# Attention's end and routing in a fused attention and expert kernel: routing split 6 and 2, last softmax ahead of the choices, a second buffer for the last values

## The chip, the cores and the metric

The kernel runs on one core of one Trainium2 chip. The core has five engines that run side by side and wait for each other by semaphores: TensorE (PE, matrix products), VectorE (DVE), ScalarE (ACT), GpSimd (POOL) and SyncE (SP, which issues transfers). The metric is device microseconds of one execution; 2% is about what its measurement tells from no change. Three runs of the kernel before gave 464.08, 466.33 and 470.67 us, a median of 466.33.

## The reference, cut to what matters

One layer over 16 sequences of 64 tokens, 256 wide (1,024 tokens). First a gated attention with a self part and a cross part, whose concatenated values are rounded to an 8-bit grid and projected. Then a mixture of 16 experts, two per token, beside one shared expert:

```python
cat = jnp.concatenate([core, xout], axis=-1)
catq = _div_clamp_fp8(cat, proj_smooth)
...
logits = flat @ router_w.T
scores = jax.nn.softmax(logits, axis=-1)
_, topk_idx = jax.lax.top_k(logits + router_bias, TOPK)
...
out = out + combine[:, e:e + 1] * (h @ Wd[e])
...
x = x + jnp.tanh(g_xattn[0]) * _L0_xattn_ref(_layernorm(x, axis=-1), ctx_2048, ...)
x = x + jnp.tanh(g_ffn[0]) * _L0_ffn_ref(_layernorm(x, axis=-1), ...)
```

The change computes the same function in another order.

## The kernel before, in words

Tokens lie in 8 tiles of 128 rows (`NT`). Attention is 32 steps (`n = 4 t + c`): four for each tile, two of self and two of cross attention, each with four heads of keys and eight of queries. A step is a software pipeline over five engines: step n's projections and statistics, the heads of step n-1, the scores and softmax of step n-2, the values, smoothing and rounding ("quantisation") of step n-3, and the output product of step n-4 are in flight together. Steps of the tiles in the middle are one loop. The last tile's steps are written out (`run_steps`), and behind them each engine's program is a list by hand: the text of the program is the order in its queue. Nothing reorders it.

The names that matter, in the order of the data. `rows_out` (L787, ScalarE) writes a tile's normalised rows, the input of the experts; `late_rows` (L1453, VectorE) does it for tile 7. `z_transposes` (L1010, TensorE) and `z_out` (L772, ScalarE) turn them into columns. `router` (L1022) makes 16 logits per token. `route_top` (L1464 to L1476, VectorE) copies the logits, adds the bias, takes the maxima and their indices, and marks the chosen experts. `ranks` (L1031, L1035, L1040, TensorE) counts how many tokens before each one chose its expert, and `route_pos` (L1504 to L1509, VectorE) turns this into the slots of the token's two rows. `twin_rows` (L581, GpSimd) makes each row's second copy. `scatter` (L591, GpSimd) sends each tile's two copies to those slots of `zbuf` in HBM, one indirect transfer per copy. All this is done in two groups, tiles 0 to 6 and tile 7 (`GROUPS`); row statistics go by three (`ROWG`).

Attention's own end stands between them: `softmax_in` (L1344, L1347), `expo` (L724), `softmax_sum` (L1353, L1356), `normalise` (L554, GpSimd), `prob_transposes` (L968), `prob_copy` (L729), `values` (L982), `over_smooth` (L1363), `quantise` (L1295 to L1306), `output` (L992). `over_smooth` writes into one buffer, `yv`, that `quantise` clips in place, so the smoothing of one step waits behind the rounding of the step before. `root` in ScalarE's steps is `roots` (L696, L698), the inverse deviation of the heads' norm, for which GpSimd's coefficients wait. The last tile's rows need its `residual` (L1377), which needs the last `output`.

When tile 7's positions are known, `block_table` (L1515 to L1526) lists 32 blocks of 128 slots. SyncE waits for all 16 scatters and loads the blocks from `zbuf` in pairs (L458). A unit is one pair: `block_transposes` (L1138), `block_rows` (L804), `unit_up` (L1098), `unit_silu` (L797), `unit_hidden` (L1534), `unit_down` (L1110, L1113), `unit_out` (L1541, L1547), and two indirect transfers to `ybuf` on GpSimd (L614). Eight shared units, one for each tile, need no table; six of them stand ahead of the blocks. At the end the two expert rows per token are loaded back, weighted and added.

## Time and profile before

| What | Value |
|---|---|
| Median of 3 runs | 466.33 us (464.08 to 470.67) |
| The profiled execution | 469.92 us, span 468.1 us |
| Busy: TensorE / VectorE / ScalarE / GpSimd | 412.9 / 370.3 / 295.6 / 285.8 us |
| Mean granted TensorE clock | 0.968 of full |
| Attention's last written-out steps and end | about 322 to 373 us |
| Expert blocks | about 397 to 450 us |

The profile is of one execution. Busy time is the time of instructions, and idle time ahead of an instruction is printed with what released it. Times in the rows are us from the span's start.
### The profile page before, as it was taken

Reading aid. Unit: us, or ns where it says so; the run is one execution under the profiler, and the core shown is the slowest. Engines: PE = TensorE matmul, PEld = TensorE weight load, DVE = VectorE, ACT = ScalarE, POOL = GpSimd, SP = SyncE. Lnnn points to the kernel's source line nnn. Section 1 sums busy time; section 2 is a strip of 40 time slices with the busy share of each in tenths; the row PEclk is TensorE's granted clock in tenths of the full one; section 3 lists DMA queues with packets and bytes.
Section 4 is the critical chain, followed back from the end, with each engine's and each line's share of the span. In section 5 each row is a group of like instructions: output and inputs, shape, how many; then the busy total and the mean of one; then the engine's idle time right before and its main releaser. Section 6 shows DMA issues by size and latency. Waiting matters only on the chain.

```text
span 468.1 us, 10277 instructions
## 1 busy us (share of the span) xinstructions
PE 412.9 (88%) x3127; PEld 314.6 (67%) x3127; DVE 370.3 (79%) x824; ACT 295.6 (63%) x622; POOL 285.8 (61%) x409
## 2 busy tenths in 40 slices
PE   0677899999999999999999999999989587999970
PEld 0444567767776776776777677677779376999960
DVE  5878889999998999999989899999985844323347
ACT  4587967777766766767776677676882122666520
POOL 2079496586867759658686775964550662367750
PEclk9999999999999999999999999999997698999995
DMA  8940909999930000000000000000094122444317
GB/s 209 269 174 3 177 13 304 248 287 267 257 83 0 0 0 0 0 0 0 0 0 0 0 0 0 0 1 1 4 404 202 63 96 81 121 129 137 104 27 242
DMA packets 34812, 45.68 MB, mean 98 GB/s; under 512 B 3034, under 2 KB 32223, under 8 KB 33888
## 3 DMA queue, kind: packets, MB, share of 16 engines
q1 hardware_dynamic: 26656, 35.61, 26.1%
q0 software_dynamic: 6992, 9.46, 9.2%
q10 hardware_dynamic: 1136, 0.27, 0.3%
q8 instruction: 14, 0.23, 0.2%
q14 instruction: 14, 0.11, 0.1%
HBM read 28.34 MB, written 24.32 MB: 113 GB/s over the span
## 4 chain that ended last, share of the span: by engine, by line
PE 34%; DVE 19%; POOL 19%; issue 15%; ACT 8%; DMA 2%; ACTq 1%; POOLq 1%; another core or an unknown queue 1%; SPq 0%; DVEq 0%
PE proj_ps L933 9%; PE score_ps L960 7%; POOL ybuf L614 4%; PE out_ps L992 4%; PE pv_ps L982 4%; POOL rot L548 3%; POOL xin L520 3%; DVE st L1336 3%; DVE yv L1363 2%; ACT rot L684 2%; PE probT_ps L968 2%; POOL reg L554 2%; PE headT_ps L951 2%; ACT qT L719 2%; PE headT_ps L1098 1%
## 5 line engine op out<-in xcount | busy, mean ns | idle before, releaser
L933 PE MATMUL proj_ps<-arena 128*128 128x512 f16 x384 | 99.4, 382 | 6.7 <-POOL arena L522 3.9
L1336 DVE BATCH_NORM_STATS2 st<-rot 128x6 f32<-128x256 f32 x192 | 72.7, 420 | 14.5 <-ACT rot L684 13.3
L684 ACT ACTIVATE rot<-proj_ps 128x512 f32<-128x512 f32 x96 | 56.4, 587 | 22.2 <-PE proj_ps L933 20.6
L548 POOL TENSOR_TENSOR rot<-rot,cw 128x512 f32<-128x512 f32 x64 | 67.3, 1072 | 2.5
L554 POOL TENSOR_TENSOR reg<-reg,rinv 128x512 f32<-128x512 f32 x32 | 34.6, 1083 | 55.5 <-DVE rinv L1356 55.5
L960 PE MATMUL score_ps<-kT,qT 128*128 128x64 f32 x512 | 62.5, 276 | 0.6 <-ACT qT L719 0.5
L960 PEld LDWEIGHTS score_ps<-kT,qT 128*128 128x128 f32 x512 | 60.6, 194 | 2.4 <-ACT qT L719 2.2
L705 ACT ACTIVATE rot<-rot,cw 128x128 f32<-128x128 f32 x128 | 40.9, 390 | 30.3 <-POOL cw L542 30.3
L933 PEld LDWEIGHTS proj_ps<-arena 128*128 (+1 forms) x384 | 37.1, 102 | 32.5 <-issue 9.0
L925 PE MATMUL proj_ps<-arena 128*128 128x512 f16 x192 | 46.7, 379 | 0.6 <-POOL arena L507 0.6
L614 POOL DMA_INDIRECT ybuf<-arena,bslot x32 | 31.4, 983 | 18.5 <-issue 13.4
L982 PEld LDWEIGHTS pv_ps<-reg,vv 64*128 64x128 f32 x512 | 32.2, 193 | 14.5 <-issue 14.0
L1363 DVE TENSOR_TENSOR yv<-pv_ps,smi 128x512 bf16<-128x512 f32 x64 | 40.7, 678 | 0.0
L982 PE MATMUL pv_ps<-reg,vv 64*128 64x128 f32 x512 | 38.5, 291 | 1.9 <-DVE yv L1363 1.9
L951 PE MATMUL headT_ps<-idf,rot 128*128 128x128 f32 x256 | 38.5, 273 | 1.2 <-ACT kT L719 1.2
L992 PE MATMUL out_ps<-wp_sb,reg 128*128 128x256 bf16 x256 | 36.0, 287 | 3.7 <-DVE reg L1306 3.7
L724 ACT ACTIVATE reg<-reg 128x512 f32<-128x512 f32 x32 | 20.1, 628 | 24.4 <-DVE reg L1347 24.4
L951 PEld LDWEIGHTS headT_ps<-idf,rot 128*128 128x128 f32 x256 | 30.3, 140 | 7.4 <-issue 1.8
L536 POOL TENSOR_TENSOR nw<-vw,r 128x12 f32<-128x12 f32 x32 | 10.3, 321 | 37.3 <-ACT r L698 37.3
L992 PEld LDWEIGHTS out_ps<-wp_sb,reg 128*128 128x128 bf16 x256 | 23.5, 102 | 11.3 <-DVE reg L1306 4.5
L925 PEld LDWEIGHTS proj_ps<-arena 128*128 (+1 forms) x192 | 18.7, 98 | 16.2 <-issue 0.8
L719 ACT ACTIVATE qT<-headT_ps,colv 128x512 f32<-128x512 f32 x32 | 24.9, 779 | 0.1
(219 smaller groups left out, 874.2 us busy)
## 6 DMA issues: line engine op xcount, KB each, us to landing
zbuf<-fill SPq DMA_DIRECT2D x1, 16576.5 KB, 66.3
arena<-in_wffn SPq DMA_DIRECT2D x4, 1536.0 KB, 13.7
arena<-zbuf SPq DMA_DIRECT2D x32, 128.5 KB
wkv_stage<-in_wkvN SPq DMA_DIRECT2D x1, 2048.0 KB, 15.3
wp_sb<-in_wpT POOLq DMA_DIRECT2D x1, 2048.0 KB, 15.8
wp_sb<-ybuf SPq DMA_DIRECT2D x8, 256.0 KB, 5.4
xs<-in_x SPq DMA_DIRECT2D x2, 512.0 KB, 5.2
vv<-in_wqN POOLq DMA_DIRECT2D x1, 1024.0 KB, 12.6
```

Of the source, the lines that this page charges most:

```text
L548: gp.tensor_tensor(r, r, cw[:, 4 * i:4 * i + 4].unsqueeze(2).to_broadcast([P, 4, D]), ALU.mult)\
L554: gp.tensor_tensor(probn[s].rearrange("p (g t) -> p g t", t=S), prob[s].rearrange("p (g t) -> p g t", t=S), rinv[:, s, :].unsqueeze(2).to_ ...
L614: gp.indirect_dma_start(ybuf, bass.IndirectOffsetOnAxis(bslot[:, 2 * s + b:2 * s + b + 1], 0), yb[s % 3][:, b, :], None, bounds_check=TOPK ...
L684: act.activation(raw[c % 2][i], proj_ps[i % 2][:, :], ACT.Copy).then_inc(proj_evac, 1)
L925: mm = pe.matmul(ps, lhs, w[:, ch, o:o + 512], start=(k == 0), stop=(k == 5))
L933: mm = pe.matmul(ps, lhs, w[kind][:, ch, 512 * b:512 * b + 512], start=(k == 0), stop=(k == 3))
L951: mm = pe.transpose(dst, raw[c % 2][i][:, h * D:(h + 1) * D], idf[:, :])
L960: mm = pe.matmul(score_ps[:, (2 * g + b) * S:(2 * g + b + 1) * S], qT[:, s, 2 * g + b, :], kT[:, s, g, b * S:(b + 1) * S], start=True, sto ...
L982: mm = pe.matmul(pv_ps[b][:, g * P:(g + 1) * P], vv[rows, u, g * D:(g + 1) * D], pT[rows, g * P:(g + 1) * P], start=True, stop=True)
L992: mm = pe.matmul(out_ps[:, 0:H], catq[u % 2][:, h * P:(h + 1) * P], wp[:, 8 * u + h, :], start=(u == 0 and h == 0), stop=(u == NU - 1 and ...
L1336: ins = ve.bn_stats(st[:, 4 * i + h:4 * i + h + 2, :].rearrange("p h s -> p (h s)"), raw[c % 2][i][:, h * D:(h + 2) * D].rearrange("p (h d ...
L1363: ins = ve.tensor_tensor(y3[:, :, b * S:(b + 1) * S], pv_ps[b][:, :].rearrange("p (h t) -> p h t", t=S), smi[:, 8 * u:8 * u + 8].unsqueeze ...
```

## The change

Five things move, all at attention's end. The routing of tiles is split otherwise: the positions and scatters go by tiles 0 to 5 and 6 to 7 (`POSG`), the maxima and choices by 0 to 5, 6 and 7 (`TOPG`); tile 7's logits lie in another bank. `route_top` becomes `route_best` (copy, bias, maxima) and `route_choice` (indices, marks), with the last softmax's sum between them. The last step's smoothed values go into `xin`, an input buffer that is free by then. In ScalarE's last step the row outputs 3 to 5 move ahead of evacuations and the root ahead of two head evacuations. The queues of all engines behind the last step are reordered to fit. The weights of the two choices are computed once for all tiles, at the end.

```diff
@@ constants
-GROUPS = [(0, 7), (7, 8)]
+TOPG = [(0, 6), (6, 7), (7, 8)]
+POSG = [(0, 6), (6, 8)]
+HOME = 7
...
+        def logits_of(t0, t1):
+            return route_ps[:, t0:t1, :] if t1 < NT else out_ps[:, H:H + NE].unsqueeze(1)
@@ GpSimd
-            def twin_rows(g):
-
-                gp.wait_ge(rows_done, GROUPS[g][1])
-                gp.tensor_copy(zrow[g][:, :, 1, 0:H], zrow[g][:, :, 0, 0:H]).then_inc(twin_done, 1)
+            def twin_rows(t0, t1):
+
+                gp.wait_ge(rows_done, t1)
+                gp.tensor_copy(zrow[0][:, t0:t1, 1, 0:H], zrow[0][:, t0:t1, 0, 0:H]).then_inc(twin_done, 1)
...
-                gp.wait_ge(twin_done, g + 1)
+                gp.wait_ge(twin_done, 2 + g)
                 gp.wait_ge(pos_done, g + 1)
-                for t in range(*GROUPS[g]):
+                for t in range(*POSG[g]):
...
             run_steps(gp, step)
+            twin_rows(0, 6)
             normalise(last - 2, 0)
-            twin_rows(0)
+            twin_rows(6, 7)
             normalise(last - 1, 1)
@@ ScalarE, step(t, c)
+                final = isinstance(n, int) and n == NU * NT - 1
                 if attend:
                     expo(n - 2, c % 2)
+                if final:
+                    rows_out(3)
+                    rows_out(4)
                 if proj:
                     evacuate(n, c, 2)
...
                 if heads:
                     heads_out(n - 1, before, 0)
+                if final:
+                    rows_out(5)
                 if proj:
                     values_out(t, c)
...
+                if final:
+                    roots(n)
                 if heads:
                     heads_out(n - 1, before, 1)
                 if heads:
                     heads_out(n - 1, before, 2)
-                if proj:
+                if proj and not final:
                     roots(n)
@@ ScalarE, behind the steps
-            for t in range(3, 6):
-                rows_out(t)
             z_out(0)
+            z_out(1)
             prob_copy(last - 3, 1)
             norm_bank0(last - 1, 3)
-            z_out(1)
+            z_out(2)
             row_root(1)
+            heads_out(last - 1, 3, 0)
             expo(last - 2, 0)
+            heads_out(last - 1, 3, 1)
+            heads_out(last - 1, 3, 2)
             rows_out(6)
-            z_out(2)
-            for i in range(3):
-                heads_out(last - 1, 3, i)
             z_out(3)
             prob_copy(last - 2, 0)
             expo(last - 1, 1)
             act.preload_act_table_set("silu_and_others")
             unit_silu(0)
+            prob_copy(last - 1, 1)
             unit_silu(1)
-            prob_copy(last - 1, 1)
@@ TensorE, behind the steps
             scores(last - 2, 0)
+            z_transposes(2)
             values(last - 3, 1)
-            z_transposes(2)
             head_transposes(last - 1, 3, 0)
+            head_transposes(last - 1, 3, 1)
+            router(0, 4)
+            head_transposes(last - 1, 3, 2)
+            router(4, 6)
+            scores(last - 1, 1)
+            z_transposes(3)
+            prob_transposes(last - 2, 0)
             output(last - 4, 0, NT - 1)
-            head_transposes(last - 1, 3, 1)
-            head_transposes(last - 1, 3, 2)
-            z_transposes(3)
-            router(0, 6)
-            prob_transposes(last - 2, 0)
-            scores(last - 1, 1)
-            router(6, 7)
             values(last - 2, 2)
             output(last - 3, 1, NT - 1)
             shared_up(0)
-            shared_up(1)
-            ranks(0)
             prob_transposes(last - 1, 1)
             values(last - 1, 3)
+            ranks(0)
+            shared_up(1)
+            router(6, 7)
             output(last - 2, 2, NT - 1)
@@ VectorE
-            def over_smooth(w, u):
+            def over_smooth(w, u, y=yv):
...
-            def quantise(w, u):
+            def quantise(w, u, y=yv):
...
             softmax_in(last - 2, 0)
+            over_smooth(last - 3, 1)
             rows_scale(1)
             softmax_sum(last - 2, 0)
-            over_smooth(last - 3, 1)
             quantise(last - 3, 1)
             softmax_in(last - 1, 1)
-            route_top(0)
+            route_best(0)
             softmax_sum(last - 1, 1)
+            over_smooth(last - 2, 2)
+            route_choice(0)
+            ve.wait_ge(xgrid_done, NT)
+            over_smooth(last - 1, 3, xin)
             route_pos(0)
-            over_smooth(last - 2, 2)
             quantise(last - 2, 2)
-            over_smooth(last - 1, 3)
-            quantise(last - 1, 3)
+            quantise(last - 1, 3, xin)
...
             index_words(1)
+            route_best(1)
+            route_choice(1)
+            route_best(2)
+            route_choice(2)
             unit_out(0)
             unit_hidden(2)
-            route_top(1)
+            route_pos(1)
             unit_out(1)
-            route_pos(1)
             block_table()
```

TensorE's queue from the last head transposes on (`score_ps` as a target of L951 and L960 is heads and scores, `proj_ps` of L1022 the logits, `pv_ps` the values; the changed kernel's line numbers are 10 higher). Before:

```order
L951 MATMUL score_ps<-idf,rot 128x2x64 x4
L951 MATMUL headT_ps<-idf,rot 128x2x64 x4
L1010 MATMUL proj_ps<-idf,wkv_stage 128x128 x2
L1022 MATMUL proj_ps<-rws,xT 128x16 x12
L968 MATMUL probT_ps<-idf,reg 128x128 x4
L960 MATMUL score_ps<-kT,qT 128x64 x8
L1022 MATMUL proj_ps<-rws,xT 128x16 x2
L982 MATMUL pv_ps<-reg,vv 128x128 x8
L992 MATMUL out_ps<-wp_sb,reg 128x256 x8
L1098 MATMUL proj_ps<-xT,arena 128x128 x8
L1098 MATMUL headT_ps<-xT,arena 128x128 x8
```

Now:

```order
L961 MATMUL score_ps<-idf,rot 128x2x64 x4
L1032 MATMUL proj_ps<-rws,xT 128x16 x8
L961 MATMUL headT_ps<-idf,rot 128x2x64 x4
L1032 MATMUL proj_ps<-rws,xT 128x16 x4
L970 MATMUL score_ps<-kT,qT 128x64 x8
L1020 MATMUL proj_ps<-idf,wkv_stage 128x128 x2
L978 MATMUL probT_ps<-idf,reg 128x128 x4
L1002 MATMUL out_ps<-wp_sb,reg 128x256 x8
L992 MATMUL pv_ps<-reg,vv 128x128 x8
L1002 MATMUL out_ps<-wp_sb,reg 128x256 x8
L1108 MATMUL proj_ps<-xT,arena 128x128 x8
L978 MATMUL probT_ps<-idf,reg 128x128 x4
```

The last scores (L960, now L970) stand ahead of tile 6's transposes, of the other step's probabilities and of tile 6's logits; one shared unit of two stands ahead of the last transposed probabilities.

VectorE's queue from the last softmax's input on (`mx` and `sm` are its maximum and sum, `m`, `i` and `chosen` the routing's maxima, indices and marks). Before:

```order
L1344 TENSOR_REDUCE mx<-score_ps 128x8
L1347 TENSOR_TENSOR reg<-score_ps,mx 128x512
L1464 COPY arena<-proj_ps 128x112
L1465 TENSOR_TENSOR arena<-arena,rowv 128x112
L1468 MAX m<-arena 128x8 x7
L1471 MAX_INDEX i<-m,arena 128x8 x7
L1473 CAST i8f<-i 128x56
L1474 TENSOR_TENSOR arena<-rowv,i8f 128x224
L1476 TENSOR_TENSOR chosen<-arena 128x112
L1353 TENSOR_REDUCE sm<-reg 128x8
L1356 RECIPROCAL rinv<-sm 128x8
L1504 TENSOR_TENSOR arena<-arena,proj_ps 128x224
```

Now:

```order
L1355 TENSOR_REDUCE mx<-score_ps 128x8
L1358 TENSOR_TENSOR reg<-score_ps,mx 128x512
L1472 COPY arena<-proj_ps 128x96
L1473 TENSOR_TENSOR arena<-arena,rowv 128x96
L1476 MAX m<-arena 128x8 x6
L1364 TENSOR_REDUCE sm<-reg 128x8
L1367 RECIPROCAL rinv<-sm 128x8
L1374 TENSOR_TENSOR yv<-pv_ps,smi 128x8x64 x2
L1484 MAX_INDEX i<-m,arena 128x8 x6
L1486 CAST i8f<-i 128x48
L1487 TENSOR_TENSOR arena<-rowv,i8f 128x192
L1489 TENSOR_TENSOR chosen<-arena 128x96
L1374 TENSOR_TENSOR xin<-pv_ps,smi 128x8x64 x2
```

The sum and its reciprocal stand between the routing's maxima and its indices, for six tiles in place of seven, and both last smoothings (L1374) are ahead of the positions.

GpSimd's queue from the normalisation ahead of the twin copy on; a row outputs' second copy is `wkv_stage<-wkv_stage`, a scatter is a DMA to `zbuf`. Before:

```order
L554 TENSOR_TENSOR reg<-reg,rinv 128x512
L581 COPY wkv_stage<-wkv_stage 128x7x256
L554 TENSOR_TENSOR reg<-reg,rinv 128x512
L591 DMA zbuf<-wkv_stage,pos 16512x257 x14
L591 DMA zbuf<-arena,pos 16512x257 x2
```

Now:

```order
L585 COPY wkv_stage<-wkv_stage 128x6x256
L558 TENSOR_TENSOR reg<-reg,rinv 128x512
L585 COPY wkv_stage<-wkv_stage 128x256
L558 TENSOR_TENSOR reg<-reg,rinv 128x512
L595 DMA zbuf<-wkv_stage,pos 16512x257 x14
L595 DMA zbuf<-arena,pos 16512x257 x2
```

The copy of six tiles stands ahead of the normalisation, that of the seventh behind it. Of the 14 scatters from `wkv_stage`, 12 now belong to the first group and two, tile 6's, wait with tile 7's for the second positions.

## Rows read from the trace of the kernel before

**Rows 1.** Chain of waits, 399 to 468 us: start us, us, what.

```profile
404.12 0.42 POOL ybuf L614
...
449.39 0.98 POOL ybuf L614
```

**Rows 2.** TensorE in order of time: start, busy us, line, tiles, [idle, releaser].

```profile
348.91 2.75 PE L1022 MATMUL proj_ps<-rws,xT 128*128 128x16 f32 x24
...
351.98 2.90 PE L960 MATMUL score_ps<-kT,qT 128*128 128x64 f32 x16
...
361.16 1.95 PE L1098 MATMUL headT_ps<-xT,arena 128*128 128x128 f32 x16
...
379.38 0.62 PE L1022 MATMUL proj_ps<-rws,xT 128*128 128x16 f32 x4
...
382.89 0.34 PE L1040 MATMUL proj_ps<-chosen,oneh 128*128 128x16 f16 x8
...
396.45 0.65 PE L1138 MATMUL pv_ps<-idf,arena 128*128 128x128 f32 x4 [0.15 <-DMA arena<-zbuf]
...
397.43 2.05 PE L1098 MATMUL proj_ps<-arena,qT 128*128 128x128 f32 x16 [0.33 <-ACT arena L804]
```

**Rows 3.** GpSimd in order of time, 338 to 404 us.

```profile
348.19 1.69 POOL L581 COPY wkv_stage<-wkv_stage 128x1792 f32<-128x1792 f32 x1
...
360.52 1.04 POOL L554 TENSOR_TENSOR reg<-reg,rinv 128x512 f32<-128x512 f32 x1 [10.64 <-DVE rinv L1356]
...
388.55 0.97 POOL L591 DMA_INDIRECT zbuf<-arena,pos  x1 [0.31 <-issue]
...
394.37 0.31 POOL L605 COPY bslot<-arena 128x1 uint32<-128x1 uint32 x2 [4.85 <-DMA arena<-zbuf]
...
396.46 0.30 POOL L605 COPY bslot<-arena 128x1 uint32<-128x1 uint32 x2 [1.78 <-DMA arena<-zbuf]
```

**Rows 4.** VectorE in order of time, 341 to 392 us.

```profile
348.32 1.84 DVE L1295 TENSOR_SCALAR yv<-yv 128x1024 bf16<-128x1024 bf16 x1
350.19 0.43 DVE L1297 TENSOR_SCALAR ya<-yv 128x1024 uint16<-128x1024 uint16 x1
...
354.91 0.69 DVE L1344 TENSOR_REDUCE mx<-score_ps 128x8 f32<-128x512 f32 x1 [2.38 <-PE score_ps L960]
...
360.23 0.20 DVE L1356 RECIPROCAL rinv<-sm 128x8 f32<-128x8 f32 x1
...
363.36 0.39 DVE L1504 TENSOR_TENSOR arena<-arena,proj_ps 128x224 f32<-128x224 f32 x1 [2.93 <-PE proj_ps L1035]
...
364.30 1.28 DVE L1363 TENSOR_TENSOR yv<-pv_ps,smi 128x512 bf16<-128x512 f32 x2
...
372.18 0.69 DVE L1306 TENSOR_TENSOR reg<-ys,ym 128x1024 bf16<-128x1024 f16 x1
...
379.94 0.43 DVE L1534 TENSOR_TENSOR arena<-proj_ps,arena 128x256 f32<-128x256 f32 x1 [1.39 <-issue]
...
381.10 0.18 DVE L1464 COPY arena<-proj_ps 128x16 f32<-128x16 f32 x1 [0.73 <-PE proj_ps L1022]
...
385.62 0.19 DVE L1504 TENSOR_TENSOR arena<-arena,proj_ps 128x32 f32<-128x32 f32 x1 [2.60 <-remote]
...
386.27 0.16 DVE L1509 SCALAR_TENSOR_TENSOR pos<-i8f,rank 128x2 uint32<-128x2 f32 x1
```

**Rows 5.** Windows: stretch, us, busy PE PEld DVE ACT POOL, PEclk, DMA share, GB/s.

```profile
352.60:359.50 6.90, 6.90 (x42) 6.21 (x42) 4.35 (x28) 2.09 (x3) 0.00 (x0) 0.51 0.59 248
...
366.30:376.50 10.20, 6.47 (x32) 4.47 (x30) 8.21 (x17) 0.23 (x2) 7.82 (x8) 0.50 0.25 90
...
390.20:393.60 3.40, 3.40 (x16) 3.23 (x15) 0.52 (x2) 0.00 (x0) 0.00 (x0) 0.50 0.28 82
```

**Rows 6.** ScalarE in order of time, 335 to 402 us.

```profile
336.61 0.60 ACT L684 ACTIVATE rot<-proj_ps 128x512 f32<-128x512 f32 x1 [0.95 <-PE proj_ps L933]
...
340.53 1.57 ACT L787 ACTIVATE wkv_stage<-xs,tn,tw 128x256 f32<-128x256 f32 x3
```

More of the change, by code:

```diff
@@ L420, in row_of @@
         def row_of(t, k):
[L421 to L422 removed]
+            return zrow[0][:, t, k, :] if t < HOME else zrow[1][:, t - HOME, k, :]
+        def logits_of(t0, t1):
+            return route_ps[:, t0:t1, :] if t1 < NT else out_ps[:, H:H + NE].unsqueeze(1)
         block = ctx.enter_context(nc.Block())
@@ L1021, in router @@
                     for c in range(HC):
-                        mm = pe.matmul(route_ps[:, t, :], zT[:, c, t * P:(t + 1) * P],
+                        mm = pe.matmul(logits_of(t, t + 1)[:, 0, :], zT[:, c, t * P:(t + 1) * P],
                                        rws[:, c, :], start=(c == 0), stop=(c == HC - 1))
@@ new lines, in route_shift, with route_weights @@
+            def route_shift():
+                link(ve.tensor_reduce(rmax[:, :], logits[:, :, :], AX.X, ALU.max))
+                ve.tensor_tensor(expd[:, :, :], logits[:, :, :], rmax[:, :].unsqueeze(2).to_broadcast([P, NT, NE]),
+                                 ALU.subtract).then_inc(rexp_in, 1)
+            def route_weights():
+                wide = [P, NT, TOPK, NE]
+                ve.wait_ge(rexp_done, 1)
+                link(ve.tensor_tensor(picked[:, :, :, :], onehot[:, :, :, :],
+                                      expd[:, :, :].unsqueeze(2).to_broadcast(wide), ALU.mult))
+                link(ve.tensor_reduce(etop[:, :, :], picked[:, :, :, :], AX.X, ALU.add))
+                link(ve.tensor_reduce(rsum[:, :], etop[:, :, :], AX.X, ALU.add))
+                link(ve.reciprocal(rsum[:, :], rsum[:, :]))
+                link(ve.scalar_tensor_tensor(coef[:, :, :], etop[:, :, :], gate[:, 1:2],
+                                             rsum[:, :].unsqueeze(2).to_broadcast([P, NT, TOPK]),
```

69 lines of the change are left out of this document (24 added, 45 removed).

## The prediction, made before the change was run

> **What bounds the kernel now.** I read the chain of waits first, then the granted clock by stretch, then TensorE, VectorE and GpSimd in order of time through 340 to 400 us. The change touches only the end of attention. In the chain, from 404 to 450 us GpSimd issues the result scatters of the expert blocks at a steady pace [rows 1]; neither those nor what follows are edited, so that stage moves as a piece with its start. Its start hangs on the first expert block's matmuls at 397.43, and the question is only how far that one instruction moves. Two things must be there for it: ScalarE's copy of the block's rows (it is named as releaser) and, just ahead on TensorE, the transposes of the second pair of blocks, which the DMA from zbuf released at 396.45, done at 397.1 [rows 2]. So the path through the scatters has about 0.4 us of slack against the other.
>
> The DMA path is a fixed series: the last slot positions are ready at 386.43, two scatters end at 389.52, the first pair of blocks is seen landed at 394.37 and the second at 396.46 [rows 3, 4]. Behind the last scatter come 6.9 us and 0.6 us of transposes whatever the order before.
>
> Ahead of the positions stands attention's end. VectorE waits 2.38 us for the last scores at 354.91, runs the routing of seven tiles for 3.2 us ahead of the last softmax's sum, so its reciprocal is ready only at 360.43, waits 2.93 us for ranks, and ends the last quantisation at 372.87 [rows 4]. TensorE was at the lower of its two clock levels, 1.2 GHz, from 352.6 to 359.5 and from 366.3 to 376.5, and again from 390.2 to 393.6 [rows 5]. Right before the first fall it had done the 24 narrow router records, 16 columns each, in 2.75 us [rows 2].
>
> **The change, step by step, against the profiled execution (469.92 us, span 468.1).**
>
> *Rows and root.* Three row outputs, 1.57 us together, leave their place behind the root; two go where ScalarE idled 0.95 us ahead of an evacuation, the third beside its wait for the values [rows 6]. What hides them is this idle time, so they cost nothing (without it, 0.5 us each). TensorE no longer waits for them with the row transposes, and the root comes two head evacuations, some 1.3 us, sooner, which the last coefficients on GpSimd follow. Late next are those head evacuations, held back 0.5 by the root: the scores that wait for them start at 340.7, which I put at 1.4 us sooner.
>
> *VectorE, at 2.4 GHz.* From 343.5: softmax input 1.4 (to 344.9), smoothing 1.2 (346.1), row scale 1.0 (347.1), sum and reciprocal 0.9 (348.0), quantisation. One such costs 3.07: two smoothings and two quantisations run from 364.30 to 372.87, 8.57 us, of which a smoothing takes 1.2 (the row's 1.28, less its overlap with what is ahead), and half of the other 6.1 is one quantisation [rows 4]. Today's one holds an instruction of 1.84 us beside 0.43 for the next of its size [rows 4], which starts while GpSimd copies the twin rows (348.19 to 349.88) and ends just after it [rows 3]. In the new order the six-tile copy is over by 344.9; a 1.04 us normalisation and a one-tile copy of some 0.3 (1.69 / 7) start with the quantisation instead [rows 3]. Bounds 0 and 1.3; I take 0.7, since they start with it and not before, which puts the end at 351.7. The Trainium skill ("SBUF — State Buffer", section "Who interferes with whom") says that whichever of the two engines comes first holds the shared port for its whole instruction and the other blocks fully. By that rule it would be the full 1.3 and every time below, the forecast too, 0.6 later; the trace of before agrees for the copy, and cannot show it for the normalisation.
>
> Then softmax input without the 2.38 us wait, since TensorE now does the last scores at 348.5 (353.1); the six maxima 1.2; the sum 0.9: reciprocal at 355.2, 5.2 us sooner. Smoothing to 356.4 and the choices, 1.8, to 358.2 lie beside GpSimd's normalisation, the transposes, ScalarE's copy and the values, which end at 358.7. The second buffer lets the last smoothing run at once, to 360.0; positions 1.0; two quantisations 6.1: 367.1. That is **5.8 us** sooner.
>
> *The clock.* TensorE's work from the last scores to the end of the first shared unit runs from 351.98 to 361.16, 9.2 us, 6.9 of it at 1.2 GHz: 5.7 at 2.4 [rows 2, 5]. Four router records leave it (0.4), and two transposes and an output join it (1.5, estimated from their records' number): 6.8 to 7.0 us, from 348.5 to 355.4, 0.9 ahead of the transposes that wait for VectorE. The 24 narrow records are still there (345.4 to 348.3) and end just where these begin. A stretch at 1.2 GHz as long as the first one now, 6.9 us, takes 3.4 us away; less the 0.9, 2.5 are lost, and up to 1.5 more if transposes and values fall in it. So 5.8 (none), 3.3 (behind slack) or 1.8 (all). I take **3.5**, nearest the middle one: the first fall came behind these very records.
>
> *From the last quantisation to the positions* there are 13.6 us now, and I keep them. Tile 6's routing (8 small instructions, 1.5 us, as tile 7's) goes into VectorE's idle time, 1.39 and 0.73 us up to 381.10 [rows 4]; where that shrinks, up to 1.0 us shows. The hidden unit and output now stand behind the choices, beside the wait for ranks of 2.6 us [rows 4]; a later ranks matmul costs nothing, only its columns double (16 to 32, beside a fixed record time).
>
> *The scatters.* The first group is 12 instead of 14, the last 4 instead of 2. On GpSimd they follow at 1.28 us each (0.97 and 0.31 of issue) [rows 3], so two more behind the last positions are **+2.6 us**. The first group would start near 361.9 to 364.5 and end by 380.2, ahead of the new positions (about 382.9), so it hides. Bounds: 0, if ScalarE or TensorE were last anyway by that much, and 2.6. Only 0.4 of slack is seen, which I take off.
>
> Sum: -3.5 + 2.6 - 0.4 = **-1.3 us**. The profiled 469.92 would be 468.6; it stands 3.6 above the median of the three runs, so the forecast is 466.33 - 1.3 = **465.0 us**. Its own range is 462.7 (5.8 gained, -3.6) to 466.7 (1.8 gained, +0.4).
>
> **Rivals.** A change of under 2% of 466.33, 9.3 us, is what this measurement can't tell from none.
>
> *Late completions go away.* At 379.38 the last router matmuls last 0.62 us and VectorE gets them only at 381.10; the ranks are recorded done at 383.24, and VectorE starts at 385.62 by a releaser that the trace doesn't name [rows 2, 4]. That is 1.1 + 2.4 = 3.5 us that no operation explains. If it belongs to this order of work, it is gone: but then the first 12 scatters (to about 380) bound the last four, and some 2.0 of the 3.5 stay. 465.0 - 2.0 = 463.0, or 460.7 with the full 5.8. Against it: the same matmuls stand there again.
>
> *Slower: the low clock moves onto the chain.* Now the last low stretch, 390.2 to 393.6, lies where 3.4 us of shared units are hidden half behind the scatters [rows 5]. Place: TensorE from the last scores to the last values, all at 1.2 GHz, and one 3.4 us stretch more on the output and shared matmuls before the positions, which are at 2.4 GHz today from 376.5 [rows 5]. Price: gain 1.8 in place of 3.5, and 1.7 to 3.4 lost: -1.8 + 2.6 - 0.4 + 2.6 = +3.0, 469.3 us. It decides as soon as the gain at the positions is below 2.2 us. For it: gaps on TensorE while VectorE does both quantisations back to back, some 2.5 and 2 us, as today's. Against it: today's stretch 366.3 to 376.5 is priced already.
>
> *Scatters are free.* ScalarE's copy decides and the four scatters hide: -3.5, 462.8 us. Against it is the row at 396.45, a wait for zbuf itself [rows 2].
>
> **Numbers.** Forecast 0.50, late completions gone 0.18, slower 0.22, free scatters 0.10. The range takes the rivals' ends in, from 460.5 to 469.5: below it are combinations of the first and third, above it a second extra low stretch. The three runs before span 464.1 to 470.7, so some of this is the kernel's own scatter. Faster by over 2% (under 457.0) needs the gain, the late completions and the scatters all at once: 0.04. Slower by over 2% (over 475.7) has no mechanism of that size in the rows: 0.03. Within: 0.93.
>
> **What would show it.** VectorE's last reciprocal of the softmax near 355 to 358, the last quantisation's end near 369.4 (367.1 with no low clock), no wait for scores over 0.5 us ahead of the last softmax; the positions near 382.9; four scatters behind them, and the first block's matmuls near 396.1, with zbuf's landing as the releaser of the transposes ahead. Wrong: if the positions come under 2.2 us sooner, or the first block waits for ScalarE alone. The sum fails most easily at the clock term.

## The result and the profile after

| | Before | The change |
|---|---|---|
| Median | 469.24 us (464.08 to 473.15, 16 runs) | 465.23 us (463.24 to 470.72, 16 runs) |
| Ratio, 95% interval | 1 | 0.9935 (0.991 to 0.996) |
| Profiled execution, span | 469.92, 468.1 us | 463.66, 461.9 us |
| Mean granted clock in it | 0.968 | 0.978 |

By the ratio the change is 3.0 us faster (1.9 to 4.2), by the two medians 4.0; the ratio leaves out executions over 1.5% above the fastest of their kernel. The forecast was 1.3. The page of the changed kernel, its first part and the clock by slice:

```profile
span 461.9 us, 10274 instructions
...
PE 410.0 (89%) x3126; PEld 313.0 (68%) x3126; DVE 368.7 (80%) x822; ACT 295.9 (64%) x621; POOL 286.2 (62%) x410
...
PEclk9999999999999999999999999999999888999995
```

The work is the same to some 3 us of busy time; the gain is in waits and in the clock. TensorE of the changed kernel in order of time, columns as in [rows 2]:

```profile
349.72 2.00 PE L970 MATMUL score_ps<-kT,qT 128*128 128x64 f32 x16
...
358.24 1.16 PE L992 MATMUL pv_ps<-reg,vv 64*128 64x128 f32 x16 [0.69 <-ACT reg L734]
...
364.43 1.05 PE L1002 MATMUL out_ps<-wp_sb,reg 128*128 128x256 bf16 x8 [2.03 <-DVE reg L1317]
...
374.51 0.52 PE L1032 MATMUL out_ps<-rws,xT 128*128 128x16 f32 x4
...
376.95 0.34 PE L1050 MATMUL proj_ps<-chosen,oneh 128*128 128x16 f16 x8
...
389.02 0.63 PE L1148 MATMUL out_ps<-idf,arena 128*128 128x128 f32 x4 [3.44 <-DMA arena<-zbuf]
...
391.83 2.68 PE L1108 MATMUL proj_ps<-arena,qT 128*128 128x128 f32 x16
```

The last scores take 2.00 us instead of 2.90 and the first block stands at 391.83 instead of 397.43 [rows 2]. Ahead of it TensorE idles 3.44 us for zbuf's rows, where before it was 0.15.

Windows of the same trace, columns as in [rows 5]:

```profile
353.00:366.00 13.00, 9.51 (x97) 8.16 (x94) 11.55 (x42) 4.58 (x7) 3.84 (x4) 1.00 0.43 177
366.00:372.80 6.80, 5.66 (x23) 4.87 (x24) 4.60 (x18) 1.69 (x3) 5.28 (x6) 0.50 0.30 107
372.80:389.90 17.10, 12.07 (x99) 11.02 (x98) 9.06 (x38) 3.48 (x9) 8.42 (x11) 1.00 0.27 93
389.90:393.30 3.40, 3.40 (x14) 2.70 (x13) 0.00 (x0) 2.13 (x4) 0.30 (x2) 0.51 0.41 122
```

The fall to 1.2 GHz in the softmax stage, at 352.6 before, is absent here; of 10.2 us at 1.2 GHz behind the quantisations 6.8 are left; the last stretch, at about the same time as before, now lies on the first block, which comes sooner, and no longer on the shared units.

VectorE in order of time:

```profile
349.09 1.15 DVE L1308 TENSOR_SCALAR ya<-yv 128x1024 uint16<-128x1024 uint16 x1
350.27 0.63 DVE L1311 TENSOR_SCALAR ym<-ya 128x1024 f16<-128x1024 bf16 x1
...
352.27 0.68 DVE L1355 TENSOR_REDUCE mx<-score_ps 128x8 f32<-128x512 f32 x1
...
355.48 0.20 DVE L1367 RECIPROCAL rinv<-sm 128x8 f32<-128x8 f32 x1
...
359.52 1.29 DVE L1374 TENSOR_TENSOR xin<-pv_ps,smi 128x512 bf16<-128x512 f32 x2 [0.90 <-PE pv_ps L992]
...
361.49 0.17 DVE L1520 SCALAR_TENSOR_TENSOR pos<-i8f,rank 128x12 uint32<-128x12 f32 x1
...
366.39 0.69 DVE L1317 TENSOR_TENSOR reg<-ys,ym 128x1024 bf16<-128x1024 f16 x1
...
375.07 0.17 DVE L1472 COPY arena<-out_ps 128x16 f32<-128x16 f32 x1 [1.27 <-PE out_ps L1032]
...
378.05 0.16 DVE L1520 SCALAR_TENSOR_TENSOR pos<-i8f,rank 128x4 uint32<-128x4 f32 x1
```

The waits of 2.38 us for the scores and 2.93 us for the ranks [rows 4] are gone. GpSimd in order of time:

```profile
348.85 1.11 POOL L558 TENSOR_TENSOR reg<-reg,rinv 128x512 f32<-128x512 f32 x1 [2.22 <-DVE rinv L1367]
350.22 0.40 POOL L585 COPY wkv_stage<-wkv_stage 128x256 f32<-128x256 f32 x1 [0.26 <-ACT wkv_stage L799]
...
362.59 1.28 POOL L595 DMA_INDIRECT zbuf<-wkv_stage,pos  x1 [5.78 <-DVE pos L1520]
...
382.84 0.97 POOL L595 DMA_INDIRECT zbuf<-arena,pos  x1 [0.30 <-issue]
388.83 0.31 POOL L610 COPY bslot<-arena 128x1 uint32<-128x1 uint32 x2 [5.02 <-DMA arena<-zbuf]
```

Sixteen scatters run from 362.59 to 383.81, 21.2 us, with one idle time of 0.77 us among them.

To lay traces beside each other I count from the start of the last values' evacuation in ScalarE's last step (338.35 us before, 339.62 in the change's first trace). "Low" is the length of the stretches at 1.2 GHz between 5 and 25 us on this count. "First" and "last positions" are the ends of the two groups' slot computations on VectorE, and "first block" is the start of its matmuls on TensorE.

| us from there | Low | Reciprocal | First positions | Last quantisation ends | Last positions | Last scatter ends | First block |
|---|---|---|---|---|---|---|---|
| before | 6.8 | 22.1 | 26.0 | 34.5 | 48.1 | 51.2 | 59.1 |
| before_again | 10.2 | 24.0 | 27.7 | 36.1 | 50.4 | 53.5 | 61.6 |
| softmax_only | 10.2 | 21.1 | 27.7 | 36.2 | 46.7 | 49.9 | 59.1 |
| the change | 0 | 16.1 | 22.0 | 27.5 | 38.6 | 44.2 | 52.2 |
| after_again | 0 | 16.1 | 22.0 | 27.5 | 43.5 | 49.1 | 56.7 |
| after_third | 3.4 | 16.2 | 23.7 | 29.1 | 40.4 | 46.0 | 53.9 |
| one_buffer | 6.8 | 17.2 | 24.1 | 31.2 | 45.5 | 51.1 | 58.8 |
| seven_one | 6.8 | 19.4 | 25.6 | 31.0 | 47.8 | 50.8 | 59.3 |
| seven_again | 0 | 16.2 | 22.5 | 27.9 | 38.4 | 44.1 | 53.1 |
| seven_filler | 0 | 16.2 | 22.5 | 27.9 | 37.1 | 44.0 | 52.7 |
| hold_scatters | 0 | 16.1 | 22.0 | 27.5 | 38.7 | 59.8 | 69.3 |
| filler | 6.8 | 16.6 | 25.3 | 30.7 | 45.8 | 51.4 | 59.7 |
| late_softmax | 3.4 | 18.0 | 23.9 | 29.4 | 45.1 | 50.7 | 59.3 |
| late_rows_root | 6.8 | 17.7 | 26.4 | 31.9 | 47.7 | 53.3 | 61.3 |

In the first pair the change is 7.1 us ahead at the last quantisation, 9.5 at the last positions, 7.0 at the last scatter, 6.9 at the first block; the span is 6.2 shorter. Over all executions the ratio gives 3.0, so this pair is a good one for the change, and the question is what the others have lost.

### The profile page after: what moved, and what is told of

The parts are those of the page before. It is cut to its first block, busy times and chain, and to the rows that moved or that the text cites. A ratio compares the mean times of both kernels' runs of the same rounds, so it can differ in the third digit from the quotient of the medians.

```text
span 461.9 us, 10274 instructions
## 1 busy us (share of the span) xinstructions
PE 410.0 (89%) x3126; PEld 313.0 (68%) x3126; DVE 368.7 (80%) x822; ACT 295.9 (64%) x621; POOL 286.2 (62%) x410
## 4 chain that ended last, share of the span: by engine, by line
PE 44%; DVE 17%; POOL 15%; issue 10%; ACT 7%; DMA 5%; POOLq 1%; ACTq 1%; SPq 0%; DVEq 0%
PE proj_ps L943 9%; PE score_ps L970 7%; PE proj_ps L1108 4%; PE pv_ps L992 4%; PE out_ps L1002 4%; POOL rot L552 4%; PE headT_ps L1108 3%; POOL xin L524 3%; DVE st L1347 3%; ACT rot L689 2%; PE headT_ps L961 2%; DMA cenf<-in_cen 2%; PE probT_ps L978 2%; POOL reg L558 2%; ACT qT L724 2%
## 5 line engine op out<-in xcount | busy, mean ns | idle before, releaser
L970 PE MATMUL score_ps<-kT,qT 128*128 128x64 f32 x512 | 61.7, 274 | 0.8 <-ACT qT L724 0.5
L970 PEld LDWEIGHTS score_ps<-kT,qT 128*128 128x128 f32 x512 | 59.7, 192 | 2.9 <-ACT qT L724 2.8
L943 PEld LDWEIGHTS proj_ps<-arena 128*128 (+1 forms) x384 | 37.1, 102 | 32.8 <-issue 9.3
L935 PE MATMUL proj_ps<-arena 128*128 128x512 f16 x192 | 46.7, 379 | 0.6 <-POOL arena L511 0.6
L992 PEld LDWEIGHTS pv_ps<-reg,vv 64*128 64x128 f32 x512 | 31.1, 187 | 13.6 <-issue 12.0
L1374 DVE TENSOR_TENSOR yv<-pv_ps,smi 128x512 bf16<-128x512 f32 x62 | 39.4, 677 | 0.0
L961 PE MATMUL headT_ps<-idf,rot 128*128 128x128 f32 x256 | 38.6, 273 | 0.4 <-ACT kT L724 0.4
L992 PE MATMUL pv_ps<-reg,vv 64*128 64x128 f32 x512 | 37.2, 285 | 0.7 <-ACT reg L734 0.7
L1002 PE MATMUL out_ps<-wp_sb,reg 128*128 128x256 bf16 x256 | 34.3, 278 | 3.7 <-DVE reg L1317 3.7
L935 PEld LDWEIGHTS proj_ps<-arena 128*128 (+1 forms) x192 | 18.7, 98 | 16.2 <-issue 0.8
## 6 DMA issues: line engine op xcount, KB each, us to landing
zbuf<-fill SPq DMA_DIRECT2D x1, 16576.5 KB, 61.3
arena<-in_wffn SPq DMA_DIRECT2D x4, 1536.0 KB, 13.6
```

What stands on the lines that cost most here:

```text
L935: mm = pe.matmul(ps, lhs, w[:, ch, o:o + 512], start=(k == 0), stop=(k == 5))
L943: mm = pe.matmul(ps, lhs, w[kind][:, ch, 512 * b:512 * b + 512], start=(k == 0), stop=(k == 3))
L961: mm = pe.transpose(dst, raw[c % 2][i][:, h * D:(h + 1) * D], idf[:, :])
L970: mm = pe.matmul(score_ps[:, (2 * g + b) * S:(2 * g + b + 1) * S], qT[:, s, 2 * g + b, :], kT[:, s, g, b * S:(b + 1) * S], start=True, sto ...
L992: mm = pe.matmul(pv_ps[b][:, g * P:(g + 1) * P], vv[rows, u, g * D:(g + 1) * D], pT[rows, g * P:(g + 1) * P], start=True, stop=True)
L1002: mm = pe.matmul(out_ps[:, 0:H], catq[u % 2][:, h * P:(h + 1) * P], wp[:, 8 * u + h, :], start=(u == 0 and h == 0), stop=(u == NU - 1 and ...
```

## The experiments

Each kernel's ratio is to the kernel before on the same chip. A kernel ran 4 to 12 times, before 25 to 35 times on each chip. The kernels of a group ran on one chip: first before_again, after_again, one_buffer and seven_one (before 478.8 us there; a scatter phase of the results that takes 48.8 us in the other groups' traces takes 53 to 56 here), then hold_scatters, filler, late_softmax and late_rows_root (before 471.43), then after_third, seven_again, seven_filler and softmax_only (before 468.88).

| | Ratio, 95% interval | Median, us |
|---|---|---|
| before_again | 0.9982 (0.9927 to 1.0037) | 480.38 |
| after_again | 0.9949 (0.9905 to 0.9992) | 475.39 |
| one_buffer | 0.9982 (0.9938 to 1.0027) | 477.32 |
| seven_one | 0.9931 (0.9897 to 0.9965) | 473.67 |
| hold_scatters | 1.0279 (1.0212 to 1.0345) | 483.37 |
| filler | 0.9958 (0.9920 to 0.9996) | 470.49 |
| late_softmax | 1.0026 (0.9992 to 1.0060) | 471.75 |
| late_rows_root | 0.9985 (0.9949 to 1.0022) | 470.30 |
| after_third | 0.9914 (0.9877 to 0.9952) | 464.61 |
| seven_again | 0.9946 (0.9902 to 0.9991) | 465.39 |
| seven_filler | 0.9932 (0.9888 to 0.9975) | 465.94 |
| softmax_only | 0.9984 (0.9953 to 1.0014) | 469.00 |

**before_again**, the kernel before, unchanged.

> The kernel before once more, unchanged, for a second trace. If the low clock in the softmax stage and the late completions belong to its order of work, the granted clock falls again near 352 us and VectorE again gets the ranks over 2 us after TensorE's record of them; the span is near 468. If they are chance, one or both are missing and the span is 462 to 466. Ratio to before 1.00 either way.

Measured: no difference from itself, with an interval 5 us wide. Its trace falls to 1.2 GHz again, for 10.2 us, this time at 350.6 us, while the 24 router records (from 348.99) are still under way. The ranks are on time here, 0.04 us behind TensorE's record; late are the transposes of the last rows, by 2.6 us, and the logits, by 1.9.

**after_again**, the change, unchanged.

> The changed kernel once more, for a second trace. If its gain lies in the order of work, the clock is at its upper level through the softmax stage again and the ratio to before is 0.991 to 0.996. If the first trace was a lucky one, a low stretch shows between 346 and 360 us and the span is 464 to 466.

Measured: 0.9949. Up to the last quantisation the trace is the first one's to 0.02 us; then it takes 16.0 us to the last positions in place of 11.1. VectorE of after_again in order of time:

```profile
366.19 0.69 DVE L1317 TENSOR_TENSOR reg<-ys,ym 128x1024 bf16<-128x1024 f16 x1
...
379.82 0.17 DVE L1472 COPY arena<-out_ps 128x16 f32<-128x16 f32 x1 [6.23 <-remote]
...
382.74 0.16 DVE L1520 SCALAR_TENSOR_TENSOR pos<-i8f,rank 128x4 uint32<-128x4 f32 x1
```

ScalarE waits ahead of that in the same manner, 4.91 us for transposes that TensorE's records show done at 373.13. So the late completions of [rows 4] can stand in the change's order too, and be larger. GpSimd stands idle 5.7 us between its two groups, and four scatters then follow the last positions where before had two: 5.6 us to their end against 3.1. That is the scatter term, 2.5 us. The first trace of the change has it too, 5.6 us from the last positions to the last scatter's end (38.6 to 44.2).

**seven_one**: the split of before, in the change's other order.

```diff
-TOPG = [(0, 6), (6, 7), (7, 8)]
-POSG = [(0, 6), (6, 8)]
+TOPG = [(0, 7), (7, 8)]
+POSG = [(0, 7), (7, 8)]
...
             output(last - 4, 0, NT - 1)
+            router(6, 7)
             values(last - 2, 2)
...
             shared_up(1)
-            router(6, 7)
             output(last - 2, 2, NT - 1)
...
-            route_best(2)
-            route_choice(2)
```

> The changed kernel with tiles 0 to 6 routed first and tile 7 alone later, as before, all other edits kept. Theory of the prediction (two more scatters behind the last positions cost 2.6 us): 1.5 to 2.6 us under the change. Theory A (the scatters stand back to back, so only their sum of 16 and their start count): equal within 0.6 us, since the two groups together end at the same time; the start is 0.3 later for the seventh tile.

Measured: 0.9931, a median of 473.67 against the change's 475.39 beside it, 1.7 us under it by the medians and 0.9 by the ratios; the intervals overlap, so this does not decide between the two expectations. Its trace had a worse clock and a stretch of 16.8 us to the last positions, and only 3.1 from there to the last scatter.

**seven_again**, the same kernel on the third chip.

> The version with seven tiles routed first once more. If late positions are the usual case (six of seven traces with scatters beside so far), two fewer scatters behind them are 1 to 2.6 us under the change on the same chip; if the first ratio (0.9931) was chance, the same within 0.5 us.

Measured: 0.9946 beside after_third's 0.9914: the other sign, overlapping again. Over both chips the split has no effect that shows. The trace says why. Here the last positions come before the first fourteen scatters are through; all sixteen stand back to back, from 23.4 to 44.1, and the two kernels' last scatters end 0.1 us apart (the change's at 44.2). With on-time positions the split changes nothing at the last scatter; where the positions are late it should (3.1 us behind them in seven_one, 5.6 in after_again), but no ratio resolves it.

**seven_filler**: seven_again with idle TensorE time filled, so that the clock stays up (an additional 31 products into a bank that is free then and overwritten later).

```diff
+            def keep_busy(n):
+                for i in range(n):
+                    pe.matmul(score_ps[:, 0:H], idb0[:, :], wp[:, i, :], start=True, stop=True)
...
+            keep_busy(18)
             output(last - 2, 2, NT - 1)
+            keep_busy(13)
             output(last - 1, 3, NT - 1)
```

> Seven tiles first, and the 18 and 13 filler products besides. If the clock behind the two last quantisations costs 1 us or more, this is 0.5 to 1.5 us under seven tiles alone and the fastest so far; if the fillers only move the fall to later, as in the trace with them alone, the same within 0.5 us.

Measured: 0.9932. The low stretch behind the quantisations is gone, and the last positions come 1.3 us sooner than seven_again's, at 37.1. The last scatter ends at 44.0 instead of 44.1. GpSimd of seven_filler in order of time:

```profile
361.85 1.28 POOL L595 DMA_INDIRECT zbuf<-wkv_stage,pos  x1 [6.03 <-DVE pos L1525]
...
380.25 0.96 POOL L595 DMA_INDIRECT zbuf<-arena,pos  x1 [0.30 <-issue]
381.52 0.96 POOL L595 DMA_INDIRECT zbuf<-arena,pos  x1 [0.30 <-issue]
```

No wait is left between them. From the first positions on GpSimd's queue is the bound, and last positions that come sooner bring nothing.

**filler**: the same in the change itself, with 16 and 13 products.

```diff
             router(6, 7)
+            keep_busy(16)
             output(last - 2, 2, NT - 1)
+            keep_busy(13)
             output(last - 1, 3, NT - 1)
```

> The changed kernel with 16 and 13 products of 256 columns into an idle bank, written over later, while TensorE waits for the last two quantisations. Theory of the clock term: no low stretch in the outputs and shared units behind them (26 us behind the last values' evacuation in both traces of the change), the last output takes 1.0 instead of 1.9 us, tile 7's columns come 1 to 2 us sooner, and the time falls by 0.5 us where the scatters stand back to back and by up to 2 us where the last positions are late. If the clock does not matter here: same within 0.5 us.

Measured: 0.9958, by its interval not to be told from the change's 0.9914 to 0.9949. The change itself was not run on this chip, and this kernel stands in for it below. Its trace fell to 1.2 GHz for 6.8 us ahead of the filler, in the softmax stage, stayed up through the outputs, and fell again at 376.5 us. It had the late completions as well, which filling TensorE's gaps thus does not remove: 15.1 us from the last quantisation to the last positions.

**hold_scatters**: no scatter ahead of the last positions.

```diff
-                gp.wait_ge(pos_done, g + 1)
+                gp.wait_ge(pos_done, 2)
```

> The changed kernel, where the first twelve scatters also wait for the last positions, so that no scatter runs beside the last rows, tile 7's routing and the shared units. Theory C (TensorE's late completions in this stretch come from the scatters' traffic beside it): between the last quantisation and the last positions no completion of TensorE is over 0.6 us behind its record, and that stretch takes 11.1 us as in the first trace of the change; the time is 10 to 14 us over the change, for twelve scatters of 1.28 us behind the positions. Theory D (they come from elsewhere, such as TensorE's instruction fetch): 2 to 6 us of late completions stay. If the scatters did not bind, the time would hardly move.

Measured: 1.0279, 13 us over before; over filler beside it 13 us by the medians and 15 by the ratios, where 10 to 14 over the change were expected. In the trace the first block starts 17.1 us later than the change's first trace. GpSimd of hold_scatters in order of time:

```profile
378.19 1.09 POOL L595 DMA_INDIRECT zbuf<-wkv_stage,pos  x1 [22.43 <-DVE pos L1520]
...
397.41 0.97 POOL L595 DMA_INDIRECT zbuf<-arena,pos  x1 [0.30 <-issue]
```

The same sixteen take 20.2 us, and the first block follows 9.5 us behind the last. With no scatter beside them, TensorE's results reach the others at once. VectorE of hold_scatters:

```profile
365.34 0.69 DVE L1317 TENSOR_TENSOR reg<-ys,ym 128x1024 bf16<-128x1024 f16 x1
...
374.12 0.17 DVE L1472 COPY arena<-out_ps 128x16 f32<-128x16 f32 x1 [1.37 <-PE out_ps L1032]
...
377.10 0.16 DVE L1520 SCALAR_TENSOR_TENSOR pos<-i8f,rank 128x4 uint32<-128x4 f32 x1
```

From the last quantisation to the last positions are 11.2 us; the three others on this chip, all with scatters beside, took 15.1 to 15.8. Once its own scatters had begun, two later completions came 1.6 and 3.6 us late. This is one trace of a thing that comes and goes between executions, so it speaks for the scatters and does not prove them. Nor does it tell the transfers' traffic from another thing that they might slow, such as the supply of TensorE's instructions: in before, TensorE itself paused three times, for 0.15 to 0.34 us, between 383.7 and 385.4, with no releaser, while its ranks were late.

**late_softmax**: the sum behind the choices.

```diff
             route_best(0)
+            route_choice(0)
             softmax_sum(last - 1, 1)
             over_smooth(last - 2, 2)
-            route_choice(0)
```

> The changed kernel with the routing's choices ahead of the last softmax's sum again. The prediction's chain: the last reciprocal 1.8 us later, and the last values, first positions and scatters with it, by 0.9 to 1.8 us; time 1 to 2 us over the change. If GpSimd's scatters were not binding: no change.

Measured: 1.0026 (0.9992 to 1.0060), 0.7% above filler beside it (0.9920 to 0.9996), so the intervals just touch; the medians are only 1.3 us apart. Against before no gain is left. The reciprocal comes 1.8 us later than in after_third, whose clock stretch is the same; the last quantisation ends only 0.25 later, since at 1.2 GHz TensorE's queue, not the reciprocal, set the values (VectorE waited 2.05 us for them there, 2.65 here). Against traces that stayed at 2.4 GHz it is 1.9. So of the 3 us by the ratio the traces account for 0.3 to 1.9. The late completions, 15.8 us to the last positions, are in its trace, but in filler's too (15.1), so they explain 0.7 at most, and the rest stays open.

**late_rows_root**: the part in ScalarE's step undone.

```diff
                 if attend:
                     expo(n - 2, c % 2)
-                if final:
-                    rows_out(3)
-                    rows_out(4)
...
-                if final:
-                    rows_out(5)
...
-                if final:
-                    roots(n)
...
-                if proj and not final:
+                if proj:
                     roots(n)
...
+            for t in range(3, 6):
+                rows_out(t)
```

> The changed kernel with ScalarE's three row outputs and the root of the last step back at their old places. The prediction: the last scores but one start 1.4 us later and the rest of attention's end follows by up to 1.4, time 0.5 to 1.4 us over the change. If the rest of the new order has slack there, the first positions move by under 0.3 us and so does the time.

Measured: 0.9985, 0.3% above filler with overlapping intervals, while the medians differ by 0.2 us the other way. In the trace the reciprocal comes 1.6 us later than the change's, first positions 4.4 (1.2 later than filler's, with the same 6.8 us of low clock).

**one_buffer**: the last smoothing waits for the quantisation again.

```diff
             route_choice(0)
-            ve.wait_ge(xgrid_done, NT)
-            over_smooth(last - 1, 3, xin)
             route_pos(0)
             quantise(last - 2, 2)
-            quantise(last - 1, 3, xin)
+            over_smooth(last - 1, 3)
+            quantise(last - 1, 3)
```

> The changed kernel with the second buffer for the last values undone: the last smoothing stands behind the rounding of the step before, and the positions of the first six tiles come ahead of it. Theory A (what binds now is GpSimd's row of 16 scatters, from the first positions on): the positions no longer wait 0.9 us for the last values nor 1.2 for their smoothing, the scatters start up to 1.2 us sooner, the first block too, and the time is 0.5 to 1.2 us under the change. Theory B (the second buffer is what brings the gain): 1 us or more over the change.

Measured: 0.9982, 0.3% above the change's 0.9949 beside it, overlapping. Its first positions come 2.1 us later than after_again's, but its trace had 6.8 us at the low clock where after_again's had none. Against filler's, with as long a stretch, they come 1.2 sooner, as Theory A had it, and the last quantisation ends 0.5 later. VectorE of one_buffer:

```profile
361.70 0.35 DVE L1515 TENSOR_TENSOR arena<-arena,proj_ps 128x192 f32<-128x192 f32 x1 [2.24 <-PE proj_ps L1045]
```

The ranks stand behind the last values in TensorE's queue, so VectorE waited for them in place of the values, and the smoothing's 1.2 us came behind the positions: the last quantisation ends 7.1 behind them instead of 5.4. With the late completions in this trace (14.3 us to the last positions) sooner first positions could not help. Which theory holds is not decided.

**softmax_only**: in the kernel before, only the sum ahead of the choices.

```diff
                 for t in range(t0, t1):
                     ins = ve.max(m8[:, t, :], biased[:, t, :])
                 link(ins)
+            def route_choice(g):
...
             route_top(0)
             softmax_sum(last - 1, 1)
+            route_choice(0)
             route_pos(0)
```

> The kernel before, with one part of the change alone: the last softmax's sum ahead of the choices of the seven tiles. In that kernel the transposes of the last probabilities stand on TensorE behind the ranks, which wait for the choices, so an earlier reciprocal should buy nothing: the reciprocal 2 us sooner, the choices 0.9 later, ratio 0.998 to 1.003. If VectorE's order alone made the gain: 0.992 to 0.996.

Measured: 0.9984 (0.9953 to 1.0014), no gain that shows, as expected. TensorE and VectorE of softmax_only:

```profile
364.67 0.21 PE L1031 MATMUL proj_ps<-chosen,trih 128*128 128x112 f16 x1
...
364.90 0.64 PE L968 MATMUL probT_ps<-idf,reg 128*128 128x128 f32 x4
```

```profile
359.32 0.20 DVE L1356 RECIPROCAL rinv<-sm 128x8 f32<-128x8 f32 x1
```

The reciprocal is ready at 359.5, 1 us sooner than before and 2.9 sooner than in before_again, whose low stretch is as long (10.2 us), but the probabilities' transposes stand behind both shared units and the ranks until 364.90. VectorE's order alone pays nothing, and late_softmax, which has all the rest, pays nothing either: as far as the intervals tell, the sum's place and TensorE's order pay only together.

**after_third**, the change on the third chip.

> The changed kernel a third time, beside the next ones on one chip: ratio to before 0.991 to 0.997. In the trace the first positions come 22.0 us behind the last values' evacuation where the clock stays up, and up to 2.5 later where it falls within 9 to 17 us of it; the last positions come 11 to 16 us behind the last quantisation, the 11 where no completion of TensorE is late.

Measured: 0.9914. No late completions in its trace (11.3 us to the last positions), 3.4 us at 1.2 GHz in the softmax stage.

## Why the prediction was right, and where its size was off

The range and the direction held, and "within 2%" too. That 465.0 meets the measured 465.23 so closely is luck: the forecast of 465.0 stood on a median of three runs, 466.33, and of 16 runs it is 469.24. Taken as a difference the forecast was 1.3 us and the result 3.0 (1.9 to 4.2), outside the interval by 0.6. In the first pair the sum up to the first block went as follows.

| Term, us | Forecast | First pair |
|---|---|---|
| Attention's end, to the last quantisation | -3.5 | -7.1 |
| From there to the last positions | 0 | -2.4 |
| Scatters behind them | +2.6 | +2.5 |
| From the last scatter to the first block | -0.4 | +0.1 |
| Sum | -1.3 | -6.9 |

Of the 6.9, 1.3 are lost ahead of the point from which I count. The first block then stands at 391.83 where 396.1 was forecast. In after_again and after_third, against the same trace of before, the sum is -2.4 and -5.2.

*Mechanism.* As described: last scores without a wait, the sum ahead of the choices, no wait for ranks. At 2.4 GHz I had the reciprocal at 355.2, first positions at 361.0, last quantisation at 367.1; the trace has 355.7, 361.7 and 367.1, in a run that stands 1.3 us later at the point from which I count.

*Attention's end, gain 3.5.* This is the step that failed, in its size: the term was mis-sized twice. With no low clock it is 7.1 us in place of 5.8: the chain from the common point on is 1.3 shorter than I had it, and 0.7 of that are the quantisations below. And I took the low clock as certain, at 2.3 us. TensorE's new order stayed at 2.4 GHz through the softmax stage in five traces of eleven (the table's Low of 0) and fell for 3.4 or 6.8 us in six; before's order fell in three of three, for 6.8 to 10.2. The price at the first positions is 1.6 us (after_third) and 3.2 (filler). So the gain at the last quantisation is 7.1, 5.4 or 3.8 us in these three against the first trace of before, in each above 3.5. The times agree: of 15 executions of the change, the ten with a mean clock of 0.973 or more average 464.6 us, the five with 0.966 to 0.970 average 466.9. What sets which one comes is not known.

*Quantisations.* The two at the end cost 5.4 us in place of 6.1. The collision measured 0.92: 1.15 and 0.63 us for two instructions of 0.43. The first ended at 350.24, 0.28 behind the normalisation (349.96), as in before it ended 0.28 behind the copy (350.16 and 349.88). The first instruction of the quantisation, 0.37 us, had started at 348.68, ahead of the normalisation at 348.85. The 0.92 lies between my 0.7 and the rule's 1.3. By the rule of the Trainium skill ("SBUF — State Buffer", section "Who interferes with whom") that whichever engine comes first blocks the other fully, the trace agrees: the 1.3 lacked only that VectorE's first instruction was there first.

*The scatters, +2.6, and the slack, -0.4.* Behind the last positions the four scatters took 5.6 us in all three traces of the change, the two of before 3.1, so as a term of the sum +2.5 is right. But it is not what the split costs. The prediction let the first twelve end by 380.2, ahead of positions at 382.9, and so charged the later two in full. The last positions came sooner than that, at 378.2, with the first group's last scatter ending at 378.26. With the old split fourteen would then have outlasted them, as they do in seven_again and seven_filler, and the end of the last scatter is the first positions and 22 us, whatever the split (22.2, 22.3, 21.7 in the change, after_third and seven_again). The other split would have paid the same 2.5 us as a wait for the queue; only with late positions (after_again) is it the split's own. The 0.4 of slack was not there: the first block followed the last scatter's end by 7.7 to 9.5 us in every trace, by 7.9 and 8.0 in the first pair.

*The 13.6 us to the last positions, kept; and "late completions go away"*, given 0.18. In the change's three traces they were 11.1, 16.0 and 11.3. So they are not a constant of the kernel, and their spread of 4.9 us is more than the forecast's whole gain at attention's end. In the first trace the late completions did go, and the rival's price was too careful: by the prediction's own times, 380.2 against positions at 379.4, the first group would have taken back 0.8 of the 3.5, not 1.5. The order did not decide it: after_again has them in the change's order, and softmax_only, with 10.5 us, has none in before's order, beside scatters. In the second group three of three traces with scatters beside have them and the one without has none; in the third group none of four; in the first all four. So they were only seen with scatters beside, on some chips or executions, and why stays open.

*"Slower"*, given 0.22, is refuted as a whole, and right as to place: a low stretch does fall on the softmax stage half the time, and costs 1.6 to 3.2 us, which the gain outweighs. *"Scatters are free"*, 0.10: half right: with on-time positions it cost nothing to move tile 6's two scatters (seven_again), but by GpSimd's queue, and not because ScalarE's copy was last.

*A loss that no step had.* The three traces of the change reach the point from which I count at 339.4 to 339.6; eleven others, among them hold_scatters and filler with the same order up to there, at 338.35 to 338.98. The loss is made in the first 11 us, where ScalarE waits for a constant to be loaded. ScalarE of the change, then of hold_scatters:

```profile
10.81 0.31 ACT L650 ACTIVATE cenb<-cenf 128x128 bf16<-128x128 f32 x1 [3.47 <-DMA cenf<-in_cen]
```

```profile
9.56 0.31 ACT L650 ACTIVATE cenb<-cenf 128x128 bf16<-128x128 f32 x1 [2.26 <-DMA cenf<-in_cen]
```

It starts at 10.7 to 10.8 in the change's three traces and at 9.4 to 9.8 in all others. So some 1 us of the gain is lost in a load that the change does not touch. Why it lands later in this kernel's traces alone, though variants ran on the same chips, is open. The variants don't carry this loss, and beside the change they look up to 1 us, 0.2%, better for it: the 0.9 us of seven_one by the ratios is no more than that.

Of the parts, by ratios: the softmax ahead of the choices is the largest (0.7%, with intervals that just touch) and works only with TensorE's new order; rows and root, and the second buffer, are each about 0.3%, and not resolved; the split of six and two shows none. No variant beat the change outside its interval.

## What to carry to other kernels

Where a queue issues at a fixed pace and its last items wait for a late input, cost a move as the later of two ends, and work it out for the earliest and the latest time that the input may have: once the queue runs without gaps, only its first item's start counts. Test each part of a bundle both ways, taken out and put in alone: a softmax moved ahead on one engine brought nothing until the engine that reads it was reordered. Look at the clock of two traces before you compare times in them, since a stretch at 1.2 GHz moved first positions by 1.6 to 3.2 us. And take the difference against as many runs of before as of after, since a median of three was 2.9 us off.

## What the runs showed of the hardware that was not expected

- TensorE's results reached VectorE or ScalarE some 1.1 to 3.9 us behind their recorded end in 8 of 14 traces while indirect scatters ran beside, and in a ninth (hold_scatters, 1.6 and 3.6 us) once its scatters had begun; in the other five, beside the same scatters, no wait for TensorE's results between 362 and 404 us ended over 0.6 us behind the record. The mechanism is open.
- The same TensorE order, with the same records before it, kept 2.4 GHz in one execution (the change's first) and fell to 1.2 GHz at 350.9 in another (after_third). Before's fall at 352.6 came 0.9 us behind the 24 narrow records, in the last scores [rows 2], before_again's in the midst of those records, and TensorE's records show no idle time in the 3.6 us ahead of before's fall, nor in the 6.9 us of its stretch [rows 5]. Filled with products, the stretch behind the quantisations stayed at 2.4 GHz in seven_filler.
- An indirect scatter of 128 rows costs GpSimd 0.97 us in most cases (up to 1.48 among the first) and 0.30 of issue, and GpSimd sees the loaded rows 4.7 to 6.2 us behind the last one's end.
